# A transformer-like layer on one core: stacks of queries and keys brought by group of pairs, and a few steps placed elsewhere in the order

## What is computed

```python
x = x + attn_a(layernorm(x), W_dq, W_uq, W_dkv, W_uk, W_uv, W_o)   # 16 heads, causal softmax, low-rank factors
x = x + ffn(layernorm(x), W_r, W_k, W_v, mu_r, mu_k)
x = x + attn_b(layernorm(x), Wq, Wk, Wv, Wo)                       # 16 heads of 8, q and k of unit length, scale 8, causal
x = x + ffn(layernorm(x), W_r, W_k, W_v, mu_r, mu_k)
# ffn(x) = sigmoid(xr @ W_r.T) * (relu(xk @ W_k.T)**2 @ W_v.T); xr, xk mix x with x of the position before
```

## Time and profile before

| what | value |
|---|---|
| median of 3 runs | 1116.97 us (1116.02 to 1117.32) |
| the profiled execution, whole | 1122.54 us |
| its span in the profile | 1120.8 us |
| TensorE busy | 959.6 us (86%) |
| VectorE busy | 878.2 us (78%) |
| ScalarE busy | 769.6 us (69%) |
| mean granted TensorE clock | 0.938 of full speed |
| DMA traffic | 112.86 MB, mean 101 GB/s |

### The profile page before, as it was taken

The page is one execution under the profiler, slowest core; times in us unless marked ns, Lnnn a source line. Parts: engine busy times, 40 slices in busy tenths (PEclk is TensorE's granted clock), DMA queues, the critical chain, the costliest instruction groups (busy, mean ns, idle before and its releaser), DMA issues.

```text
span 1120.8 us, 36161 instructions
## 1 busy us (share of the span) xinstructions
PE 959.6 (86%) x15409; PEld 524.1 (47%) x15409; DVE 878.2 (78%) x2112; ACT 769.6 (69%) x1042; POOL 281.6 (25%) x264
## 2 busy tenths in 40 slices
PE   3668777979898989999999999899989999899694
PEld 1324344445454545555544545455544545455353
DVE  3757885779788898998989898989898898765632
ACT  2137464757677778777777888777877778688671
POOL 6011212212213123232323232222323232222212
PEclk8569898989998999999999999999999999899897
DMA  6155235425815427181817254362819062505130
GB/s 137 39 106 116 69 68 114 101 61 119 183 27 135 114 72 178 48 193 40 195 35 187 53 150 99 95 155 68 182 39 202 19 178 53 121 7 124 59 66 19
DMA packets 86145, 112.86 MB, mean 101 GB/s; under 512 B 13152, under 2 KB 79840, under 8 KB 79840
## 3 DMA queue, kind: packets, MB, share of 16 engines
q1 hardware_dynamic: 85984, 110.55, 41.5%
HBM read 55.22 MB, written 54.53 MB: 98 GB/s over the span
## 4 chain that ended last, share of the span: by engine, by line
PE 46%; DVE 30%; ACT 12%; issue 7%; DMA 2%; POOL 1%; SPq 0%; POOLq 0%; DVEq 0%; ACTq 0%
PE acc L722 16%; DVE rowmax L1074 12%; ACT prob L923 8%; PE pool L705 7%; PE pool L636 4%; PE pool L749 3%; PE pool L755 3%; DVE xn L1032 2%; PE pool L777 2%; PE pool L601 2%; PE pool L652 2%; DVE stats L1020 2%; PE pool L763 2%; PE pool L674 2%; DVE rest_k L1045 2%
## 5 line engine op out<-in xcount | busy, mean ns | idle before, releaser
L923 ACT ACTIVATE prob<-pool 128x1024 f32<-128x1024 f32 x576 | 565.5, 1029 | 150.5 <-PE pool L652 146.1
L1074 DVE TENSOR_REDUCE rowmax<-pool 128x2 f32<-128x1024 f32 (+7 forms) x480 | 357.8, 792 | 92.9 <-PE pool L652 89.9
L722 PE MATMUL acc<-prob,vals_a 128*32 128x512 f32 (+7 forms) x2048 | 169.3, 426 | 0.2 <-ACT prob L923 0.2
L722 PE MATMUL acc<-prob,vals_b 128*32 128x512 f32 (+7 forms) x2048 | 166.4, 426 | 1.2 <-DVE turned_b L1109 0.7
L636 PE MATMUL pool<-stack_ka,stack_qa 48*64 48x512 bf16 (+7 forms) x2048 | 118.7, 305 | 47.3 <-issue 13.9
L705 PE MATMUL pool<-stack_qa,stack_ka 51*64 51x512 bf16 (+7 forms) x2048 | 113.7, 302 | 31.3 <-DVE rowmax L1074 18.2
L705 PE MATMUL pool<-stack_qb,stack_kb 48*64 48x512 bf16 (+7 forms) x2048 | 113.7, 298 | 23.4 <-ACT prob L923 9.7
L652 PE MATMUL pool<-mask_t,ident_b 64*64 64x128 bf16 (+1 forms) x2304 | 130.7, 216 | 1.8 <-issue 1.8
L636 PEld LDWEIGHTS pool<-stack_ka,stack_qa 48*64 48x64 bf16 x2048 | 42.8, 109 | 141.0 <-ACT prob L923 59.3
L1284 POOL TENSOR_TENSOR rstd<-mv,minus_half 128x4 f32<-128x4 f32 x64 | 65.4, 1021 | 153.1 <-DVE mv L1027 153.1
L1296 POOL TENSOR_TENSOR parts_q<-rest_q,parts_q 128x512 bf16<-128x512 f32 x32 | 37.1, 1158 | 186.7 <-DVE parts_q L1048 186.6
(11 more groups left out here) (129 smaller groups left out, 1386.6 us busy)
## 6 DMA issues: line engine op xcount, KB each, us to landing
stack_qa<-scratch_qa SPq DMA_DIRECT2D x32, 384.0 KB, 7.9
stack_ka<-scratch_ka SPq DMA_DIRECT2D x32, 384.0 KB, 7.8
stack_kb<-scratch_kb SPq DMA_DIRECT2D x32, 384.0 KB, 5.6
stack_qb<-scratch_qb SPq DMA_DIRECT2D x32, 384.0 KB, 6.9
scratch_qa<-parts_q SPq DMA_DIRECT2D x16, 384.0 KB, 3.6
scratch_ka<-parts_k SPq DMA_DIRECT2D x16, 384.0 KB, 6.2
scratch_qb<-parts_q SPq DMA_DIRECT2D x16, 384.0 KB, 2.6
scratch_kb<-parts_k SPq DMA_DIRECT2D x16, 384.0 KB, 2.6
```

Of the source, the lines that this page charges most:

```text
L722: last = eng.matmul(acc[32 * j:32 * j + 32, BLK * blk:T], vals[a][:, blk, GROUP * g + j, :], prob[n % NPROB][:, k, at:at + T - BLK * blk], ...
L923: eng.activation(prob[n % NPROB][:, :, :], place["unit", n][0][:, :, :], ACT.Exp, scale=scale).then_inc(S["exped"], 1)
L1074: last = eng.tensor_reduce(to, of, axis=AX.X, op=ALU.max)
```

## The change

- `restack` is called with a group `g` in place of a tensor `n`. The first call brings queries and keys of group 0 (four DMAs of 48 rows by 4 pairs, 192 KB each), the second those of group 1. The two slots of `restack_a` and of `restack_b` stay. Each group has semaphores of its own (`stacked_qa0`, `stacked_qa1` and so on). Where a stack tile was used before, the wait is for the last unit of scores of that group instead of the whole attention.
- `row_maxima` and `attend` wait for the stacks of their own group alone. `split` waits for both groups before it overwrites `scratch`.
- `values_b` moves from slot -35 to -37 in the entries `None` and 2 (sequences 2 to 13).
- Of `row_maxima0`, entry `None`: unit 0 from -59 to -59.2, unit 4 from -48 to -46.8, unit 6 from -44 to -42.8; the last also in the entries -2 and -1.

```diff
     None:
-        "row_maxima0": [-59, -56, -55, -51, -48, -46, -44, -36, -36],
+        "row_maxima0": [-59.2, -56, -55, -51, -46.8, -46, -42.8, -36, -36],
...
-        "values_b": [-35, -35],
+        "values_b": [-37, -37],
...
     2:
-        "values_b": [-35, -35],
+        "values_b": [-37, -37],
...
     -2:
-        "row_maxima0": [-60, -58, -55, -51, -47, -46, -44, -36, -36],
+        "row_maxima0": [-60, -58, -55, -51, -47, -46, -42.8, -36, -36],
...
     -1:
-        "row_maxima0": [-60, -58, -56, -51, -46, -44, -44, -36, -36],
+        "row_maxima0": [-60, -58, -56, -51, -46, -44, -42.8, -36, -36],
...
-            for what in ("projected_", "part0_", "rest_", "part1_", "part2_", "written_", "stacked_"):
+            for what in ("stacked_" + n + str(g) for g in range(GROUPS)):
+                S[what] = ctx.enter_context(nc.semaphore("s_" + what))
+            for what in ("projected_", "part0_", "rest_", "part1_", "part2_", "written_"):
...
-            for k, n in enumerate("qk"):
-                yield e.restack(b, n, "a"), [max(at("restack_a")[k], front[-1] + 1, end_a[2] + k)]
+            for k in range(GROUPS):
+                yield e.restack(b, k, "a"), [max(at("restack_a")[k], front[-1] + 1, end_a[2] + k)]
...
-            for k, n in enumerate("kq"):
-                yield e.restack(b, n, "b"), [max(at("restack_b")[k], back[-1] + 1, of_b - 2 * SLOTS + k)]
+            for k in range(GROUPS):
+                yield e.restack(b, k, "b"), [max(at("restack_b")[k], back[-1] + 1, of_b - 2 * SLOTS + k)]
...
             def row_maxima(self, b, g, units):
                 eng, q = self.eng, self.q
-                q.wait_ge(S["stacked_qa"], 32 * (b + 1))
-                q.wait_ge(S["stacked_ka"], 32 * (b + 1))
+                q.wait_ge(S[f"stacked_qa{g}"], 32 * (b + 1))
+                q.wait_ge(S[f"stacked_ka{g}"], 32 * (b + 1))
...
-                        q.wait_ge(S[f"stacked_q{a}"], 32 * (b + 1))
-                        q.wait_ge(S[f"stacked_k{a}"], 32 * (b + 1))
+                        q.wait_ge(S[f"stacked_q{a}{g}"], 32 * (b + 1))
+                        q.wait_ge(S[f"stacked_k{a}{g}"], 32 * (b + 1))
...
-                    q.wait_ge(S[f"stacked_{n}{a}"], 32 * b)
+
+                    for g in range(GROUPS):
+                        q.wait_ge(S[f"stacked_{n}{a}{g}"], 32 * b)
...
-            def restack(self, b, n, a):
-                eng, q = self.eng, self.q
-                to = stack[n + a][b % len(stack[n + a])]
-                if n + a == "ka":
-                    q.wait_ge(S["ones_rows"], min(2 * b + 2, 4))
-
-                b_ = b - len(stack[n + a])
-                if b_ >= 0:
-                    q.wait_ge(S["scored"], unit_of[a, b_][-1] + 1)
-                q.wait_ge(S[f"written_{n}{a}"], 48 * (b + 1))
-                for r in range(2):
-                    src = scratch[n + a].rearrange("t (d r a) c -> (t d) r (a c)", d=D, r=2)[:, r, :]
-                    eng.dma_start(to[BLK * r:BLK * r + ROWS, :, :].rearrange("p a c -> p (a c)"),
-                                  src).then_inc(S[f"stacked_{n}{a}"], 16)
+            def restack(self, b, g, a):
+                eng, q = self.eng, self.q
+
+                for n in "qk" if a == "a" else "kq":
+                    to = stack[n + a][b % len(stack[n + a])]
+                    if n + a == "ka":
+                        q.wait_ge(S["ones_rows"], min(2 * b + 2, 4))
+
+                    b_ = b - len(stack[n + a])
+                    if b_ >= 0:
+                        q.wait_ge(S["scored"], unit_of[a, b_][9 * g + 8] + 1)
+                    q.wait_ge(S[f"written_{n}{a}"], 48 * (b + 1))
+                    for r in range(2):
+                        src = scratch[n + a].rearrange("t (d r a) c -> (t d) r a c", d=D, r=2)
+                        eng.dma_start(to[BLK * r:BLK * r + ROWS, GROUP * g:GROUP * g + GROUP, :],
+                                      src[:, r, GROUP * g:GROUP * g + GROUP, :]).then_inc(S[f"stacked_{n}{a}{g}"], 16)
                 yield
```

## The result

The changed kernel takes 1099.92 us (median of 4 runs, 1095.18 to 1102.09), the one before 1116.49 beside it (4 runs, 1113.40 to 1117.32). The ratio is 0.9851, with an interval of 0.9813 to 0.9888: faster by 16.6 us.

A forecast was written before the change was run, and what follows sets the result against it. TensorE was taken to set the pace, with three early stops waiting for stack bytes. Stops -14.1 and clock -1.5 sum to -15.6, from 1116.97 to 1101.4 us; own range 1096 to 1107, 8 in 10 range 1092 to 1113.

The forecast's parts named there:

- What was waited for: At TensorE's three early stops, stack bytes are waited for; half are group 1's, which the first nine units don't read.
- Stops one and three: TensorE idle 13.93 us before the first row maxima and 4.29 us before the first scores of attention b.
- half the bytes, not half the time: Rival, chance 0.12: part of a DMA's time doesn't shrink with its bytes; gain 7 us, total 1110.
- the stacks aren't what is waited for: Rival, chance 0.04: two of three waits have no name; little changes or 4.96 alone is won, 1112 to 1117.
- The two rivals on the values: Moved values_b: ScalarE waits go, 8 us more, 1093 (0.13); or copies ahead of exponentials become the limit, 1120 (0.09).
- The three stops: First maxima, sequence 1's maxima, first scores of attention b: gains of 5.1, 4.8 and 4.2 us, sum 14.1.
- The clock: TensorE's low clock behind the third stop (1.9 us) and second (0.6) goes; 1.5 counted, bounds 0 and 2.5.
- second stop: TensorE idle 4.96 us before the row maxima of sequence 1, waiting for a DMA into stack_ka; gain 4.8 us.
- strict reading: Skill's warning that idle gaps return the clock to its low level; taken strictly it gives the whole 1.9 us.
- Price of more DMAs: 128 more DMAs, 3.3 us of SyncE a turn, in its slack: no cost on the path; upper bound 51 us.
- Moved slots: values_b and units of maxima: taken as 0; bounds -8 to +19 for values, 3 us either way for maxima.
- announced signs: Profile after: first maxima at 26 to 27 us, stops gone, same 15 us lead at every later point, turns 60.85 +- 0.2.

The follow-up runs named there:

- Groups waited for together: Against the kernel before: DMAs by group, old slots, but TensorE waits for both groups wherever it waits for stacks; 1111.59 us, ratio 0.9951.
- groups alone: The changed kernel with the slot table of the kernel before; 1094.61 us, ratio 0.9801, and again 1097.38 us, ratio 0.9829.
- the filler: Kernel before plus 78 products of 128 columns, results overwritten, before the wait for the first scores of attention b; 1116.94 us, ratio 1.0008.
- the small size in the old order: Against the kernel before: 256 DMAs of 192 KB issued tensor by tensor, TensorE waiting for both groups, old slots; 1119.70 us, ratio 1.0038.
- portions for the first group: DMAs by group with old slots, plus sequence 0's group 0 in two portions, pairs 0 and 2 first; 1094.97 us, ratio 0.9815.

## Why the prediction was right

**What was waited for: right.** Stops one and three had no name in the trace. Groups waited for together have them back with the name of the stack's DMA, and when each group is waited for alone they are short or gone. The rivals "half the bytes, not half the time" and "the stacks aren't what is waited for" are out: the start is at 26.27, not near 30. The two rivals on the values are out as well: a turn changed by 0.1 to 0.2 us, not by the 0.7 and 1.3 that they need.

**The three stops: 14.1 forecast, 14.4 measured.** To keep single executions from weighing, I take the mean of the two traces of groups alone against the mean of the two of before.

| place | before | groups alone | lead | new lead | forecast |
|---|---|---|---|---|---|
| first maxima, sequence 0 | 31.25 | 26.13 | 5.1 | 5.1 | 5.1 |
| maxima, sequence 1 | 72.10 | 61.35 | 10.8 | 5.6 | 4.8 |
| values of a, sequence 1 | 101.29 | 88.84 | 12.5 | 1.7 | 0.6 (clock) |
| first scores of b, sequence 0 | 192.76 | 176.57 | 16.2 | 3.7 | 4.2 |
| end of b, sequence 0 (`x_b` written) | 239.50 | 221.05 | 18.5 | 2.3 | 1.9 (clock) |

The stops' new leads sum to 14.4. For the first start, bytes over rate agree with the means to 0.1 us, but single pairs of traces give 4.4 to 5.9. At the other two places TensorE hardly waits any more (0.34 us at most in these traces), so they show that the stop is gone and not the rate. The 3.7 is uncertain by itself: from the values of sequence 1 to the first scores of attention b the eight traces without the third stop take 86.5 to 90.7 us, the five with it 90.4 to 92.9.

One reading under the 4.8 is off. The prediction counts both tensors of sequence 1, 1.57 MB, from 62.6 us. But the queries' DMAs had been issued at 59.74, and from 62.6 on 132 GB/s were moved, which is 1.29 MB up to 72.4:

```profile
59.74 1.10 SPq L1453 DMA_DIRECT2D stack_qa<-scratch_qa  x2
```

```profile
62.60:72.40 9.80, 4.95 (x53) 1.34 (x45) 1.14 (x9) 3.83 (x5) 1.01 (x1) 0.67 0.88 132
```

**The clock: undersized.** Of 0.6 + 1.9 the prediction counted 1.5, with a bound of 2.5; the rows show 1.7 + 2.3 = 4.0. The step that failed is "after the second stop VectorE's reductions are the limit": there too TensorE's 0.64 us a product had been a cost. That the second of the two is the clock's is backed by the filler. The first is read from the traces alone, but from all 14. From the first maxima of sequence 1 to its values of attention a, six of the eight that wait for a group take 26.76 to 26.78 us, with a granted clock of 1.00 from 64 to 76 us. The other two take 28.22 and 29.44, with 0.74 and 0.50 for part of it. The six with the second stop take 28.45 to 29.73, with 0.50 behind it. The Trainium skill ("TensorE: Matmul & The Clock Gate", Why this matters for your kernels) warns of idle gaps between bursts of products. The prediction named its strict reading and then counted less; these runs agree with the strict one.

**Price of more DMAs: the sign was wrong.** 0 was taken. When both groups are waited for, order and size together are worth 5.3 us, and the small size in the old order costs 2.7, so the order is worth some 8. Part of that is the clock's, since the stops get shorter (2.99 us for the third, and 6.91 us behind it instead of 8.71 and 8.11). The prediction took the flow of 160 GB/s as given; it depends on the order of issue. With half the bytes waited for, it has less to act on, and the first start shows none of it.

**Moved slots: 0 forecast, about 3 us lost.** Alone they cost 3.5 us (ratio 1.0032, 1.0015 to 1.0050). With groups, the mean of 9 runs of the changed kernel in both measurements is 1099.5, that of 10 runs of groups alone 1096.3: 3.2 us (0.7 to 5.8 by the spread of these runs), inside bounds of -8 to +19 for the values and 3 either way for the maxima. In the steady turn the working was partly right. The wait for `ffn_prod` that was worked out came, 0.35 us a turn. But the result for the values alone is +0.12 us (60.97 to 60.85), not -0.1, the maxima alone give -0.13, and both together -0.22: they don't add. So the loss must lie outside the turns. They win 1 us from sequence 6 to 13: 425.09 and 424.69 in the two traces of the changed kernel, where one turn is 60.95 each, against 425.82 and 425.94 with groups alone. Where the loss lies the traces didn't settle. There is a hint: behind the values of attention a of sequence 13, the three traces with groups and moved `values_b` take 285.3 to 288.0 us, the four with groups throughout and `values_b` at -35 take 283.8 to 284.8. But before alone varies there from 284.25 to 287.60.

**The sum.** Groups are worth 20.4 us by all ten runs (mean 1096.3, of the 41 runs of before beside them 1116.7), of which 18.5 are found up to 240 us; the last 2 are not placed. Less the 3.2 for the slots that is 17.2, where 16.6 was measured. The forecast of 15.6 had the main term right to 0.3. That the total came within 1.0 us is luck beyond that: a gain that it undersized (clock) and a loss that it put at nothing (slots) have opposite signs. Of its announced signs all came but one: the lead isn't the same 15 us from the third stop on, but grows from 17.7 at sequence 3 to 22.8 at the end, since the clock of single executions adds to it up to 400 us. The turns, 60.63, lie at the edge of their 60.85 +- 0.2. Of the kernels that ran, groups with the old slots is the best (1094.61 and 1097.38), with portions for the first group at least no worse (1094.97).

## What to carry to other kernels

When an engine stands still for data, ask which bytes the next instructions read, and bring and wait for only those first; bytes over the rate of that very stretch gave the first gain, 5.1 us, as the mean of two traces. Price each stop with the slow products behind it, not only with its idle time. When several edits come as one, time them apart even if the total fits the forecast: here one part cost 3 us that another part paid for.

## What the runs showed of the hardware

- **The order of issue changes what the same DMAs cost.** 256 DMAs of 192 KB took 37.7% of the engines' span when the two halves of the rows and the two tensors alternated, 41.9% when two pieces of one half came in a row. In time: 1111.59 and 1119.70 us. Which of the two alternations counts is open. The Trainium skill ("DMA: Bandwidth & Descriptors", Rules for kernel authors) says of two transfers to disjoint partition halves that they serialize, and advises against them. Here, where this kernel has two, their order mattered; one transfer of all rows was not tried.
- **The same program is granted different clocks.** The kernel before took 1112.17 to 1121.77 us in 23 runs, and its two traces differ by 5.8 us, with 0.90 and 1.00 of the clock from 300 to 350 us. Differences of single traces under some 5 us are not to be read as the change's, but most steady turns repeat to 0.02 us.
- **A stop costs again behind itself.** Behind 3.7 to 5.5 us of standing still (second stop) the same work took 28.45 to 29.73 us, without a stop and at a granted clock of 1.00 it took 26.77. Behind 3.5 to 4.3 us (third stop) it took 46.4 to 47.1 us instead of 44.2 to 45.0.
- **Filling a stop keeps the clock up, and gains nothing if it runs over**: 78 products turned 8.71 and 8.11 us into 5.82 behind them, and started them 1.6 to 2.0 us late.
